# Both low-rank projections as fp32 products on four column groups, with the slots of a hand-dealt recurrence kernel dealt anew

## The reference

```
def layer0(x, a1, b1, a2, b2):                        # RANK = 8, per batch
    u   = einsum('btd,bdr->btr', x, a2)               # projection to rank 8
    mid = x @ base_down + einsum('btr,blr->btl', u, b2)
    mid = gelu(mid)
    v   = einsum('blr,btl->btr', b1, mid)             # projection to rank 8
    return x + mid @ base_up.T + einsum('bkr,btr->btk', a1, v)
x = x + layer0(x)
def layer1(x):                                        # scan over the 512 times
    xW = x @ Wx + b
    h_t = tanh(xW_t + h_{t-1} @ Wh)
x = x + layer1(x)
```

## Time and profile before

| | |
|---|---|
| time, median of 3 runs | 1256.99 us (1255.58 to 1260.54) |
| the profiled execution | 1258.02 us |
| its span | 1256.3 us |
| PE busy | 1206.2 us (96%) |
| DVE busy | 914.0 us (73%) |
| ACT busy | 627.6 us (50%) |
| POOL busy | 280.2 us (22%) |
| the chain that ended last | PE 89%, DMA 5%, ACT 2%, DVE 2% |
| mean granted TensorE clock | 0.985 of full speed |

### The profile page before, as it was taken

One profiled execution on the slowest core, in us unless ns is written; L12 is line 12 of the kernel. 1 busy time (PEld: TensorE's weight loads), 2 busy tenths in 40 slices (PEclk: granted clock), 3 DMA queues, 4 the chain that ended last, 5 costly groups with the idle time before them and its releaser, 6 DMA issues.

```text
span 1256.3 us, 49350 instructions
## 1 busy us (share of the span) xinstructions
PE 1206.2 (96%) x20408; PEld 988.1 (79%) x20408; DVE 914.0 (73%) x3675; ACT 627.6 (50%) x2433; POOL 280.2 (22%) x523
## 2 busy tenths in 40 slices
PE   6778999999999999999999999999999999999996
PEld 5345788888888888888888888888888888888764
DVE  4444577878777787878787787878787777877564
ACT  2122455555555555555555545555555555554442
POOL 0000122222222222222222222222222222222111
PEclk9799999999999999999999999999999999999998
DMA  7998211312121211212121112213121211001022
GB/s 236 396 409 271 32 20 19 53 19 45 28 36 25 35 32 27 45 20 48 24 41 30 31 26 36 36 19 53 19 44 28 38 31 32 11 14 25 2 36 35
DMA packets 284078, 75.63 MB, mean 60 GB/s; under 512 B 273072, under 2 KB 273088, under 8 KB 283856
## 3 DMA queue, kind: packets, MB, share of 16 engines
q1 hardware_dynamic: 277488, 71.89, 24.4%
q10 hardware_dynamic: 6368, 0.60, 0.4%
HBM read 55.68 MB, written 16.78 MB: 58 GB/s over the span
## 4 chain that ended last, share of the span: by engine, by line
PE 89%; DMA 5%; ACT 2%; DVE 2%; SPq 1%; issue 1%; ACTq 0%; DVEq 0%; POOLq 0%; POOL 0%
PE bulk L949 44%; PE rec L965 32%; PE bulk L938 5%; PE bulk L952 5%; DMA work<-in_L_cond_W_dram 4%; ACT hf L607 1%; PE bulk L927 1%; SPq L447 1%; DVE z L830 1%; ACT rec L547 1%; PE bulk L887 1%; DMA hf<-in_L_cond_b_dram 0%; DVE work L797 0%; DVE wx_s L669 0%; ACT work L580 0%
## 5 line engine op out<-in xcount | busy, mean ns | idle before, releaser
L965 PEld LDWEIGHTS rec<-hs,wh_s 128*128 128x128 f16 x16352 | 442.7, 96 | 128.8 <-DVE hs L838 125.7
L607 ACT ACTIVATE hf<-z,scl 128x32 f32<-128x32 f32 x1024 | 273.9, 315 | 484.7 <-DVE z L830 480.2
L965 PE MATMUL rec<-hs,wh_s 128*128 128x32 f16 x16352 | 493.4, 177 | 6.9 <-ACT rec L547 6.9
L502 POOL TENSOR_TENSOR work<-work,hf 128x64 f32<-128x64 f32 x512 | 278.8, 544 | 966.4 <-DVE hs L838 966.4
L830 DVE TENSOR_REDUCE z<-rec 128x32 f32<-128x96 f32 x1022 | 231.1, 256 | 113.1 <-PE rec L965 99.7
L835 DVE TENSOR_SCALAR hs<-hf 128x32 f16<-128x32 f32 x1024 | 181.6, 177 | 105.9 <-ACT hf L607 105.9
L838 DVE SCALAR_TENSOR_TENSOR hs<-hf,hs 128x32 f16<-128x32 f32 x1024 | 197.3, 193 | 35.3
L949 PE MATMUL bulk<-act_x,down_s 128*128 128x512 f32 x768 | 219.0, 408 | 2.8 <-ACT work L580 2.8
L949 PE MATMUL bulk<-mid_s,up_s 128*128 128x512 f32 x768 | 217.6, 406 | 0.0
L949 PE MATMUL bulk<-act_s,wx_s 128*128 128x512 f32 x768 | 207.4, 407 | 0.0
L547 ACT ACTIVATE rec<-work 128x32 f32<-128x32 f32 x1022 | 183.7, 210 | 0.0
(11 more groups left out here) (105 smaller groups left out, 751.2 us busy)
## 6 DMA issues: line engine op xcount, KB each, us to landing
work<-in_L_cond_W_dram SPq DMA_DIRECT2D x33, 1024.0 KB, 9.0
work<-in_x_dram SPq DMA_DIRECT2D x256, 64.0 KB, 3.3
out_dram<-work SPq DMA_DIRECT2D x248, 64.0 KB, 2.4
work<-in_L_cond_base_up_dram SPq DMA_DIRECT2D x1, 1024.0 KB, 7.8
work<-in_L_cond_base_down_dram SPq DMA_DIRECT2D x1, 1024.0 KB, 10.6
work<-in_L_cond_Wh_dram SPq DMA_DIRECT2D x1, 1024.0 KB, 13.0
work<-in_L_cond_Wx_dram SPq DMA_DIRECT2D x1, 1024.0 KB, 9.2
out_dram<-work ACTq DMA_DIRECT2D x8, 64.0 KB, 3.2
```

What stands on the lines that cost most here:

```text
L502: nc.gpsimd.tensor_tensor(xs, xs, hf[:, t % 4], ALU.add).then_inc(sum_done, 1)
L607: nc.scalar.activation(hf[:, t % 4, half], z[:, half], ACT.Tanh, scale=inv).then_inc(tanh_done, 1)
L965: last = nc.tensor.matmul(R[fo][:, m, 0:PARTS, :], wh_s[:, q, k, n * P:(n + 1) * P], hs[:, k, :, :], start=(m == k == q == 0), stop=(k == ...
```

## The change

The projection products take fp32 operands as they are, x (`x1`) or the GELU's output (`gel`, now kept for all four tiles), and the unsplit factors `a2_f`, `b1_f`. The array's columns are used as four groups of 32: group j multiplies the 32 factor columns of four batches with the 128 columns of the same four batches. Both projections are one block in one slot: U_SLOT is -2 and V_SLOT 10. What comes out is 128 partitions x 128 columns; VectorE selects from it with one small mask, rounds in four pieces of 32 x 128 and subtracts in four. ScalarE's copy (`both`) is gone, and so are the high and low parts of eight of the sixteen factor tiles. The tables of MID, OUT and XW are new; XT_AT, XHI_AT, XLO_AT, X1LO_SLOT and Y_SLOT are as before. The u block waits for the transposed x alone; the low parts of x are waited for by the mid products.

```
-U_SLOT = (-2, -2, -2, -1)
-V_SLOT = (10, 10, 10, 11)
-MID_SLOTS = (-1, (0.6,) + (1,) * 10)
-OUT_SLOTS = (11, (0.6,) + (1,) * 10)
-XW_SLOTS = (22, (1,) * 8)
+U_SLOT = -2
+V_SLOT = 10
+MID_SLOTS = (-1, (1,) * 11)
+OUT_SLOTS = (11, (1,) * 10 + (0.5,))
+XW_SLOTS = (21, (0.5,) + (1,) * 8)
...
+        a2_f = sb("a2_f", [P, KT, B * RANK])
+        b1_f = sb("b1_f", [P, KT, B * RANK])
...
+        gel = sb("gel", [P, KT, COLS])
+        rank = sb("rank", [P, JC])
...
             for e in "uv":
-                s[e + "b"] = s[e][-1]
-                s[e + "a"], s[e + "sel"], s[e + "lo"] = [s[e][-1] + j for j in (1, 2, 3)]
+                s[e + "sel"], s[e + "lo"] = s[e] + 1, s[e] + 2
...
-                for e, slot, mm, bank in ((0, at["ub"], u_mm, BANK_U), (1, at["vb"], v_mm, BANK_V)):
-                    if r == slot:
-                        act.wait_ge(mm, n + 1)
-                        need(act, rank_sel, 2 * n + e)
-                        nc.scalar.copy(both[:], bulk[P // 2:P, bank, :]).then_inc(rank_low, 1)
...
-                    if r == at[name + "a"]:
-                        dve.wait_ge(rank_low, 2 * n + e + 1)
-                        nc.vector.tensor_tensor(both[:], both[:], bulk[0:P // 2, bank, :], ALU.add).then_inc(rank_sum, 1)
                     if r == at[name + "sel"]:
-                        dve.wait_ge(rank_sum, 2 * n + e + 1)
-                        nc.vector.copy_predicated(rank[:], mask[:], both[:]).then_inc(rank_sel, 1)
+                        dve.wait_ge(mm, n + 1)
+                        need(dve, rank_done, 2 * n + e)
+                        nc.vector.copy_predicated(rank[:], mask[:], bulk[:, bank, 0:JC]).then_inc(rank_sel, 1)
...
-                        nc.vector.tensor_copy(rank_s[0:P // 2, :], rank[:]).then_inc(rank_rnd, 1)
+                        for j in range(COLG):
+                            last = nc.vector.tensor_copy(rank_s[j * SQ:(j + 1) * SQ, j * JC:(j + 1) * JC],
+                                                         rank[j * SQ:(j + 1) * SQ, :])
...
                     if r == at[name + "lo"]:
-                        nc.vector.tensor_tensor(rank_s[P // 2:P, :], rank[:], rank_s[0:P // 2, :].bitcast(F32),
-                                                ALU.subtract).then_inc(rank_done, 1)
+                        for j in range(COLG):
+                            low = (j * SQ + P // 2) % P
+                            last = nc.vector.tensor_tensor(
+                                rank_s[low:low + SQ, j * JC:(j + 1) * JC], rank[j * SQ:(j + 1) * SQ, :],
+                                rank_s[j * SQ:(j + 1) * SQ, j * JC:(j + 1) * JC].bitcast(F32), ALU.subtract)
...
-            def rank_in(out_bank, fac_s, src, k):
-                for g in range(GROUPS):
-                    for a in (HI, LO):
-                        last = nc.tensor.matmul(bulk[:, out_bank, g * GC:(g + 1) * GC], fac_s[:, k, g, :],
-                                                src[:, a, k, g * GC:(g + 1) * GC], start=(k == g == a == 0),
+            def rank_in(out_bank, factor, src):
+                for k in range(KT):
+                    for j in range(COLG):
+                        last = nc.tensor.matmul(bulk[j * SQ:(j + 1) * SQ, out_bank, 0:JC],
+                                                factor[:, k, j * SQ:(j + 1) * SQ], src[:, k, j * JC:(j + 1) * JC],
...
-                for k in tile_at(sched(n)["u"], r):
-                    pe.wait_ge(xlo_done, n * KT + k + 1)
+                if r == sched(n)["u"]:
+                    pe.wait_ge(x_tr, (n + 1) * KT)
...
-                for k in tile_at(sched(n)["v"], r):
-                    pe.wait_ge(mid_done, n * KT + k + 1)
+                if r == sched(n)["v"]:
+                    pe.wait_ge(gel_f, (n + 1) * KT)
```

90 lines of the change are left out of this document (38 added, 52 removed).

## The result

| | before | after |
|---|---|---|
| time, median of 4 runs | 1256.78 us (1255.58 to 1260.54) | 1289.3 us (1288.92 to 1290.31) |
| span of the profiled execution | 1256.3 us | 1287.2 us |
| one chunk in the middle | 69.60 us | 72.29 us |
| start of the first recurrence step | 143.71 us | 134.91 us |
| PE / DVE / ACT busy | 96 / 73 / 50% | 93 / 71 / 47% |

The ratio of after to before is 1.0254, interval [1.0236, 1.0273]: slower, as forecast (1298), by 32.5 us instead of 41.

The account below looks back on a forecast made before the run. TensorE was taken to bound every step, with the chain and VectorE close behind. Per chunk -1.7 + 1.35 + 2.44 + 0.87 = +3.0 us, fifteen chunks +45, less 4.4 at the start: 1298 us, range 1264 to 1319.

Parts of the forecast that it names:

- A: Projections on TensorE: 32 products per chunk go, two steps hold a projection alone; gain 1.7 us per chunk.
- B: Step 22: an xw product moved a step earlier waits for the third low part of x1; loss 1.35 us per chunk.
- C: Steps 0, 1, 12, 13: VectorE's small casts and subtractions wait for each other when partitions change; loss 2.44 us per chunk.
- Rivals 1 and 2: VectorE's small pieces overlap without waiting (1267 us, chance 0.10); or run beside each other (1260 or 1248 us, chance 0.09).
- D: Other collisions of the new slot deal, in step 11, positions 15 and 18, and step 26; loss 0.87 us per chunk.
- E: Start of the recurrence: without ScalarE's copy chunk 0's evictions run earlier, first step at 139.3 us; gain 4.4 us, once.
- Rival 3: Idle stretches in steps 22, 12 and 13 drop TensorE to half clock for 3.4 us per chunk: 1323 us, chance 0.07.
- Rival 4: The projection's column groups do not run side by side; its step takes 4.8 us, total 1380 us, chance 0.02.

Follow-up runs that it names:

- the kernel with spread pieces: Changed kernel with slot tables dealt anew and the selection's nine operations spread over four positions from the second chunk on: 1227.74 us, ratio 0.9765 to the kernel before.
- The tables run: Changed kernel with only its slot tables dealt anew (x~ W1 products from 22, transposition out of step 12, out products 11 to 21): 1255.71 us, ratio 0.9986.

## Why the prediction was right, and where it was off

**A, TensorE's work.** Forecast 1.7; 1.74 is left as the remainder, and the kernel with spread pieces gives 1.73. The W2 blocks of the earlier trace rows were the right row: where nothing else is waited for, at the start of the recurrence, the next product follows the first of the 32 instructions after 1.01 us (131.41 to 132.42), against the 1.00 taken. The 1.09 us of step 10 (588.97 to 590.06) contain a wait for the split. That the steps are set by the chain is also shown by the run with a quarter of the projection. Step 10 is 0.06 shorter than forecast: the two GELUs ahead of its tanh push it by 0.07 (1.17 us into the step, against 1.10 in step 30), where 0.13 was taken.

**B, the low part.** Forecast 1.35, measured 1.36, and with the half position undone the chunk lost 1.24. The working went by when VectorE makes the third low part; that the table of X1LO stayed where it was, while the product that needs it moved a step ahead, was all of it.

**C, the small pieces.** Forecast 2.44, measured 2.32. The mechanism was the one read off the single case of the earlier trace rows: the run with all pieces on one set of partitions removed the wait, the run with them spread over four positions removed its price. Two sizes were off. The gap between pieces is 0.013 us, not the 0.03 assumed, and the selection takes 0.30, not 0.34. What the sum did not have is the contention with GpSimd, which the prediction had only in its range: 0.07 us on one subtraction here, 0.15 where the pieces overlap. Two places of the working do not add up as written. For step 0, 0.60 less 0.12 is 0.48 and not 0.46. For step 12, 0.05 + 1.35 + 0.70 - 0.80 is 1.30 us late and not 1.06. The trace has 1.04, because the selection starts 0.11 before the step does (592.15 against 592.26) and the reduction 0.63 after the transposition (593.47 to 594.10); so the number used was good, and its working was not shown. Rivals 1 and 2 fall with it: no two small operations ran beside each other beyond the 0.07 to 0.08 us of overlap.

**D, the collisions.** Forecast 0.87, measured 0.75. Only step 26 was mis-sized, 0.17 instead of 0.25; its loss went alone when step 25 got its sixth product back. The tables run removed those of steps 16 and 19 as well, together. That of step 11 stays in every run (2.18 to 2.19), so its cause, the low part of the last GELU tile, is argued and not shown by an experiment.

**E, the start.** Forecast 4.4, measured 8.8. The copy's price came out right: put back it costs 4.1 us. There is luck in this, since forecast and measurement both contain the half clock behind the idle stretch, and the repeated trace of before is without it. From the first eviction to the first step pass 5.4 us, where the forecast has 5.1 (134.2 to 139.3). The step that failed is the assumption that everything ahead of it stays where it was: the xw products, taken to stand where they did, came earlier, and with them the first eviction by 4.7 us (129.5 against 134.2). Of this 2.4 us are the W2 blocks, which belong to the program and have no cause found. Some 1.6 us are the products at half clock from 119.6 to 123 in the first trace of before, which belong to that execution. The last 0.7 us are a size: the first eviction starts 1.9 us before the projection's first product (131.41), where 1.2 was taken. A single trace of before could not tell the second. Against the repeated trace of before the start is 6.6 us earlier and not 8.8.

**The sum.** From its first step to its last the recurrence grew by 39.3 us (forecast 45; a middle chunk by 2.69 instead of 3.0, the first and the last of the fifteen with next work by 2.2 and 2.1), the start gave 8.8, and the difference is 30.5 us; with 0.4 behind the last step it makes the 30.9 us between the two spans. The forecast of 1298 is high by 8.7: 5.7 from the chunks, 4.4 from the start, and 1.4 us the other way, mostly because the medians lie 32.5 us apart and the spans 30.9.

**Rival 3, the clock.** It did not come true: the granted clock is 1.00 in the step that idles 1.08 us and over steps 12 and 13, and no fall of it is on record in after from 51 to 1217 us. **Rival 4** is refuted by the 1.08 us of step 10.

## What to carry to other kernels

When products move a slot earlier, look up for each of them when its operands are made; here one half position let TensorE wait 1 us in every chunk, and cost more than half of the loss. Small operations of VectorE are to be counted by what they hold up, about 0.24 (a cast) to 0.3 us (a subtraction) each when they change partitions, not by their elements, and spread so that no step has more than its spare time. A change that saves work on the engine that is the bound pays only while the other engines' work in the same steps stays within their spare time: with the same arithmetic, 32 us lost became 30 us won by where things stand.

## What was not expected of the hardware

- A VectorE operation with two inputs (32 x 128, 277 ns alone) took 433 ns where a GpSimd addition of 128 x 64 ran beside it; with the GpSimd operation cut to one column it took 277 again. Casts, which have one input, meet the addition too: of the three in the kernel with spread pieces the middle one takes 320 ns and the others 217 and 223. The Trainium skill (SBUF — State Buffer, Who interferes with whom) has it that a VectorE instruction with two SBUF inputs contends with a GpSimd instruction that reads SBUF, and that their shared port is an exclusive lock. The trace agrees that they collide. At first sight it speaks against a lock, since the subtraction that began at 562.37 was over at 562.80, only 0.14 us after the addition (562.27 to 562.66), and not 0.28. But only a part of the 277 ns grows with the columns: 684 ns at 512 columns (L780) and 277 at 128 make 1.06 ns a column, an estimate of 0.14 us for 128. So the times fit a subtraction that has done the rest and waits with its columns until the addition is over. The spans of GpSimd are rough, so this is no proof either way.
- An idle stretch of TensorE of about 2.8 us in the same place was followed by half clock in one trace of before and in the run with the copy, and by full clock in the other trace of before. The idle stretches of 1.08 us in the changed kernel, with products around them, were not followed by it in any chunk.
